# A four-block transformer kernel: residual with tokens on partitions, norms by bn_stats, key copies on ScalarE, and a new order

## The reference, cut to what matters

```
x = x + sigmoid(silu(c @ gate_w1) @ gate_w2) * (routed @ out_w)     # block 0, c = [norm(x), evidence, cond]
for each of blocks 1, 2, 3:                                        # eps, gates and biases differ
    n = ln(x) * (1 + scale_a) + shift_a                            # scale, shift, gate: one vector per sequence
    x = x + gate_a * (softmax(q(n) @ k(n).T * s) @ v(n) @ w_proj + b)
    x = x + (softmax(q(ln(x)) @ k(ctx).T * s) @ v(ctx) @ w_cproj + b)
    n = ln(x) * (1 + scale_m) + shift_m
    x = x + gate_m * (gelu(n @ w1 + b1) @ w2 + b2)                 # ln(t) = (t - mean) / sqrt(var + eps) over the 128 features
```

## Time and profile before

| | |
|---|---|
| median of 3 runs | 2806.82 us |
| the profiled execution, time | 2816.98 us |
| the profiled execution, span | 2815.2 us |
| granted TensorE clock, mean | 0.984 |
| instructions | 76312 |
| busy: PE / DVE / ACT / POOL | 2544.6 / 2204.7 / 1906.7 / 0.2 us |

### The profile page before, as it was taken

One profiled execution on the slowest core, in us unless ns is written; L12 is line 12 of the kernel. 1 busy time (PEld: TensorE's weight loads), 2 busy tenths in 40 slices (PEclk: granted clock), 3 DMA queues, 4 the chain that ended last, 5 costly groups with the idle time before them and its releaser, 6 DMA issues.

```text
span 2815.2 us, 76312 instructions
## 1 busy us (share of the span) xinstructions
PE 2544.6 (90%) x32150; PEld 1948.2 (69%) x32150; DVE 2204.7 (78%) x3752; ACT 1906.7 (68%) x3901; POOL 0.2 (0%) x4
## 2 busy tenths in 40 slices
PE   4989999999998999989999899989999898998997
PEld 3766777667766777667777667766777666776665
DVE  3788887788778887778877888777887778768785
ACT  2666667766676667767677666776667776777765
POOL 0000000000000000000000000000000000000000
PEclk9999999999999999999999999999999999999999
DMA  6100000000000000000000000000000000000000
GB/s 125 35 2 2 2 19 18 13 2 4 24 13 11 2 7 20 16 8 2 13 18 18 2 2 13 24 13 2 2 13 24 13 2 2 11 15 9 2 2 9
DMA packets 57963, 37.63 MB, mean 13 GB/s; under 512 B 20192, under 2 KB 52768, under 8 KB 57632
## 3 DMA queue, kind: packets, MB, share of 16 engines
q1 hardware_dynamic: 49120, 32.72, 4.1%
q10 hardware_dynamic: 8512, 0.03, 0.2%
HBM read 28.44 MB, written 4.29 MB: 12 GB/s over the span
## 4 chain that ended last, share of the span: by engine, by line
PE 59%; DVE 27%; ACT 8%; issue 3%; DMA 1%; DVEq 0%
PE pair L540 16%; PE pair L548 12%; PE pair L585 7%; DVE mx L731 7%; DVE wide L733 7%; PE pair L601 6%; PE pair L570 6%; PE pair L606 5%; PE pair L614 4%; DVE wide L727 3%; PE pair L555 2%; ACT vb L654 2%; ACT wide L661 2%; DVE xn L689 1%; DVE xn L691 1%
## 5 line engine op out<-in xcount | busy, mean ns | idle before, releaser
L585 PE MATMUL pair<-konst,wide 128*128 128x128 f32 x3072 | 404.5, 277 | 107.4 <-DVE wide L733 90.6
L661 ACT ACTIVATE wide<-pair 128x1024 f32<-128x1024 f32 x384 | 386.7, 1021 | 163.6 <-PE pair L585 162.3
L585 PEld LDWEIGHTS pair<-konst,wide 128*128 128x128 f32 x3072 | 347.6, 142 | 183.3 <-DVE wide L733 139.9
L731 DVE TENSOR_REDUCE mx<-pair 128x16 f32<-128x1024 f32 x320 | 389.3, 1216 | 49.3 <-PE pair L570 48.9
L733 DVE TENSOR_TENSOR wide<-pair,mx 128x1024 f32<-128x1024 f32 x320 | 391.8, 1224 | 10.9
L654 ACT ACTIVATE vb<-pair 64x128 f32<-64x128 f32 x768 | 207.6, 270 | 43.1 <-PE pair L555 26.5
L540 PE MATMUL pair<-wide,konst 128*128 128x256 f32 x704 | 218.4, 401 | 17.2 <-ACT wide L634 13.2
L570 PE MATMUL pair<-km,qT 32*64 32x256 f32 x6144 | 217.0, 390 | 17.6 <-DVE wide L733 7.1
L601 PEld LDWEIGHTS pair<-wide,vb 128*32 128x32 f32 x12288 | 183.9, 110 | 68.3 <-issue 29.0
L601 PE MATMUL pair<-wide,vb 128*32 128x64 f32 x12288 | 213.7, 221 | 11.0 <-ACT wide L661 9.2
L669 ACT ACTIVATE rec<-pair 128x256 f32<-128x256 f32 x192 | 73.7, 384 | 217.7 <-PE pair L606 217.3
(11 more groups left out here) (224 smaller groups left out, 4601.7 us busy)
## 6 DMA issues: line engine op xcount, KB each, us to landing
km<-probs_by_expert SPq DMA_DIRECT2D x32, 384.0 KB, 3.4
rows<-in_x_dram SPq DMA_DIRECT2D x32, 128.0 KB, 2.2
rows<-in_ctx_dram SPq DMA_DIRECT2D x32, 128.0 KB, 2.3
out_dram<-wide SPq DMA_DIRECT2D x32, 128.0 KB, 1.8
w0e<-in_L_xcond_e_w_dram SPq DMA_DIRECT2D x4, 384.0 KB, 5.7
w1fc<-in_L_xcond_fc_w_dram SPq DMA_DIRECT2D x2, 256.0 KB, 5.6
w2fc<-in_L_xcond_W_mlp_dram SPq DMA_DIRECT2D x2, 256.0 KB, 6.9
wide<-in_L_xcond_ffn_w_dram SPq DMA_DIRECT2D x2, 256.0 KB, 5.4
```

Of the source, the lines that this page charges most:

```text
L585: ins = pe.transpose(b[:, t:t + 128], G.ss[:, 2 * c + rr, a:a + 128], ident)
L661: act.activation(G.pT[:, :, 4 * c:4 * c + 4, :].rearrange("k p h q -> k p (h q)"), two_banks(name)[:].rearrange("k (p n) -> k p n", p=2), ...
L731: dve.tensor_reduce(top, heads(s), AX_X, ALU.max).then_inc(*tick("dve", ("max", G.n, tag, c)))
```

## The change

Four things change together.

**The residual has tokens on partitions.** `x` is now 128 tokens x 2 x 128 features, loaded and stored without any turn; only the context is still turned. There are two x buffers per stream. The cross projections, block 3's self projection and block 3's last MLP product swap their operands (`pe_token_product`), so that the result has tokens on partitions and is added to x from PSUM by one pass. Gated deltas are still made with features on partitions; a piece `bk` turns them back with two transposes ahead of the add. A bias along features can't ride on the add any more: for three of the adds GpSimd adds a bias row to x earlier, after the norm has read x.

**Norms by bn_stats.** VectorE takes mean and variance per token (two `bn_stats`, two `bn_aggr`), ScalarE takes logarithm and exponential of 128 x 2 numbers, VectorE subtracts and multiplies (two `tensor_scalar` over 128 columns), TensorE transposes twice, and ScalarE evicts: with scale and shift in four activations of 64 columns, one per sequence, or in one of 256 columns.

**Masked key copies on ScalarE.** Four activations of 256 columns with the mask as scale and the masked bias as bias.

**The order.** Most costs of the timetable are changed a little, a hop towards TensorE has its own length, GpSimd is an engine of the timetable, and each kind of piece has an offset on its rank from the table `ORDER` (some 200 numbers, of which one line stands below). In the order that comes out ScalarE has 241 table loads where it had 294.

```diff
 assert GI == NG
 PE_MM, PE_TURN, PE_SCORES, PE_MIX = 0.44, 0.12, 1.05, 1.95
-ACT_256, ACT_BIAS, ACT_SBUF, ACT_1024, ACT_VALUES, ACT_TABLE = 0.36, 0.45, 0.42, 0.96, 1.2, 1.3
-DVE_256, DVE_PTR, DVE_1024, DVE_MASK, DVE_SMALL = 0.36, 0.42, 1.16, 1.24, 0.2
-HOP, PE_HOP, LEAD = 0.07, 0.22, 12.0
+ACT_256, ACT_BIAS, ACT_SBUF, ACT_1024, ACT_VALUES, ACT_MODULATE, ACT_TABLE = 0.34, 0.43, 0.42, 0.95, 1.08, 1.0, 1.3
+POOL_ADD, ACT_KEYS = 0.8, 1.55
+DVE_256, DVE_PTR, DVE_1024, DVE_MASK, DVE_SMALL, DVE_TWO, DVE_STATS, DVE_APPLY = 0.36, 0.42, 1.195, 1.24, 0.16, 0.95, 0.75, 0.42
+HOP, TO_PE_HOP, PE_HOP, LEAD = 0.07, 0.16, 0.24, 11
+ORDER = {
+    "in": -8, "c in": -8.5, "pen": 54.5, "rstd0": 9.5, "ap0": 55, "nT0": 10, "xn0": 22,
...
-        rank = {p.name: p.name[0] * LEAD - left[p.name] for p in pieces}
+        rank = {p.name: p.name[0] * LEAD - left[p.name] + ORDER.get(p.name[1], 0.0) for p in pieces}
...
-                self.x, self.cT = own("x", [128, T]), own("cT", [128, T])
+                self.x = own(f"x{n // NS % 2}_", [128, TT, D])
+                self.ctx, self.cT = own("ctx", [128, TT, D]), own("cT", [128, T])
+                self.stats, self.mv, self.rstd = own("stats", [128, 2, TT, 6]), own("mv", [128, 2, TT, 2]), own("rstd", [128, 2, TT])
...
+        def pe_token_product(pe, name, pairs):
+
+            b = claim(pe, name)
+            for t in range(TT):
+                for i, (m, w) in enumerate(pairs):
+                    ins = pe.matmul(b[:, t * 128:(t + 1) * 128], m[:, t * 128:(t + 1) * 128], w, start=(i == 0), stop=(i == len(pairs) - 1))
+            ins.then_inc(*tick("pe", ("mm", name)))
+
...
+        def dve_stats(dve, G, tag):
+
+            x, stats, mv, _, _ = norm_of(G, tag)
+            for t in range(TT):
+                dve.bn_stats(stats[:, t, :], x[:, t, :]).then_inc(*tick("dve", ("stats", G.n, tag, t)))
+            for t in range(TT):
+                dve.wait_ge(*done("stats", G.n, tag, t))
+                dve.bn_aggr(mv[:, t, :], stats[:, t, :]).then_inc(*tick("dve", *([("var", G.n, tag)] if t else [])))
...
+        def dve_apply(dve, G, tag):
+
+            x, _, mv, rstd, out = norm_of(G, tag)
+            dve.wait_ge(*done("rstd", G.n, tag))
+            for t in range(TT):
+                dve.tensor_scalar(out[:, t, :], x[:, t, :], mv[:, t, 0:1], rstd[:, t:t + 1], ALU.subtract, ALU.mult)\
+                    .then_inc(*tick("dve", *([("normed", G.n, tag)] if t else [])))
+
...
+        def act_modulate(act, G, tag, scale, shift, dst):
+
+            name = (G.n, tag, "n")
+            act.wait_ge(*done("mm", name))
+            for q in range(GB):
+                seq = G.n * GB + q
+                act.activation(dst[:, q * S:(q + 1) * S], tile(name)[:, q * S:(q + 1) * S], ACT.Identity,
+                               scale=table[:, scale, seq:seq + 1], bias=table[:, shift, seq:seq + 1])\
+                    .then_inc(*tick("act", *([("free", name), ("xn", G.n, tag)] if q == GB - 1 else [])))
+
...
-        def dve_keys(dve, G, tag, bias):
-
-            mask = konst[:, K_MASK:K_MASK + JH].unsqueeze(2).broadcast_to((128, JH, T))
-            wide = lambda ap: ap.unsqueeze(1).broadcast_to((128, JH, T))
+        def act_keys(act, G, tag, bias):
+
+            masks = konst[:, K_MASK:K_MASK + JH]
+            name = (G.n, tag, "k")
             if bias is None:
-                dve.tensor_tensor(G.km[:], wide(G.kT[:]), mask, ALU.mult).then_inc(*tick("dve", ("km", G.n, tag)))
+                act.wait_ge(*done("kT", G.n, tag))
+                src = G.kT[:]
             else:
-                name = (G.n, tag, "k")
-                dve.wait_ge(*done("mm", name))
-                dve.scalar_tensor_tensor(G.km[:], wide(tile(name)[:, 0:T]), bias, mask, ALU.add, ALU.mult)\
-                    .then_inc(*tick("dve", ("free", name), ("km", G.n, tag)))
+                act.wait_ge(*done("mm", name))
+                src = tile(name)[:, 0:T]
+            for j in range(JH):
+                end = [("km", G.n, tag), *([] if bias is None else [("free", name)])] if j == JH - 1 else []
+                act.activation(G.km[:, j, :], src, ACT.Identity, scale=masks[:, j:j + 1],
+                               bias=0.0 if bias is None else kbias[:, 4 * bias + j:4 * bias + j + 1]).then_inc(*tick("act", *end))
...
+        def pool_bias(pool, G, which, ready, end):
+
+            pool.wait_ge(*done(*ready))
+            pool.tensor_tensor(G.x[:], G.x[:], bias_tok[:, which:which + 1, :].broadcast_to((128, TT, D)), ALU.add).then_inc(*tick("pool", ("biased", G.n, end)))
+
+        def dve_residual(dve, G, name, biased, end):
+
+            name = (G.n, *name)
+            if biased:
+                dve.wait_ge(*done("biased", G.n, end))
+            dve.wait_ge(*done("mm", name))
+            dve.tensor_tensor(G.x[:], tile(name)[:, 0:T].rearrange("p (t d) -> p t d", t=TT), G.x[:], ALU.add)\
...
-        def norm(G, tag, before, ready, scale, shift, dst, eps, src):
-
-            cen, var = (tag, "cen"), (tag, "var")
-            put_product(G, "cen" + tag, cen, PE_MM, [(center, src[:])], before, wait=[ready])
-            put(G, "sq" + tag, "act", ACT_256, lambda act: act_square(act, G, tag), "cen" + tag)
-            put_product(G, "var" + tag, var, PE_MM, [(average, squares(G, tag)[0])], "sq" + tag, wait=[("sq", G.n, tag)])
-            put(G, "rstd" + tag, "act", ACT_BIAS + ACT_SBUF, lambda act: act_rstd(act, G, tag, eps), "var" + tag, gives=[var], table=EXP_TABLE)
+        def norm(G, tag, before, ready, scale, shift, dst, eps):
+
+            def dve_first(dve):
+                if ready is not None:
+                    dve.wait_ge(*ready)
+                dve_stats(dve, G, tag)
+            put(G, "st" + tag, "dve", DVE_STATS, dve_first, *before)
+            put(G, "rstd" + tag, "act", 0.48, lambda act: act_rstd(act, G, tag, eps), "st" + tag, table=EXP_TABLE)
+            put(G, "ap" + tag, "dve", DVE_APPLY, lambda dve: dve_apply(dve, G, tag), "rstd" + tag)
+            put(G, "nT" + tag, "pe", 2 * PE_TURN, lambda pe: pe_turn_norm(pe, G, tag), "ap" + tag, takes=[((tag, "n"), 1)])
             if scale is not None:
-                put(G, "scale" + tag, "dve", DVE_256, lambda dve: dve_scale(dve, G, tag, scale, dst), "sq" + tag, gives=[cen])
-                put(G, "xn" + tag, "dve", 2 * DVE_256 + HOP, lambda dve: dve_norm(dve, G, tag, shift, dst), "rstd" + tag, "scale" + tag)
-            elif tag == "0":
-                put(G, "xn" + tag, "dve", 2 * DVE_256 + HOP, lambda dve: dve_norm0(dve, G), "rstd" + tag, gives=[cen])
+                put(G, "xn" + tag, "act", ACT_MODULATE, lambda act: act_modulate(act, G, tag, scale, shift, dst), "nT" + tag, gives=[(tag, "n")])
             else:
-                put(G, "xn" + tag, "dve", DVE_256, lambda dve: dve_norm(dve, G, tag, None, dst), "rstd" + tag, gives=[cen])
+                put(G, "xn" + tag, "act", ACT_BIAS if tag == "0" else ACT_256, lambda act: act_normed(act, G, tag, dst), "nT" + tag, gives=[(tag, "n")])
+
+        def add_gated(G, src, tag, before, ready):
+
+            def emit(pe):
+                pe.wait_ge(*done(*ready))
+                pe_turn_back(pe, (G.n, tag, "back"), src)
+            put(G, "bk" + tag, "pe", 2 * PE_TURN, emit, before, takes=[((tag, "back"), 1)])
+            put(G, "x" + tag, "dve", DVE_256, lambda dve: dve_residual(dve, G, (tag, "back"), False, tag), "bk" + tag, gives=[(tag, "back")])
...
-            put(G, "km" + tag, "dve", DVE_MASK + (3 * DVE_256 + HOP if L == 3 else 0), dve_k, "k" + tag, gives=[(tag, "k")])
+            if L == 3:
+                put(G, "kT" + tag, "dve", 3 * DVE_256 + HOP, lambda dve: dve_rotary(dve, G, tag, "k", G.kT, "kT"), "k" + tag, gives=[(tag, "k")])
+            put(G, "km" + tag, "act", ACT_KEYS, lambda act: act_keys(act, G, tag, bias), "kT" + tag if L == 3 else "k" + tag,
+                gives=[] if L == 3 else [(tag, "k")])
...
```

More of the change, by code:

```diff
@@ L440, in _ @@
                 pe.wait_ge(*done("router pad"))
-                pe.transpose(bank[7][:, 0:B], G0.x[:, 0:D], ident).then_inc(*tick("pe", ("cond",)))
+                pe.transpose(bank[7][:, 0:B], visits[NS].x[:, 0, :], ident).then_inc(*tick("pe", ("cond",)))
                 for n, (w, i) in enumerate(blocks):
@@ L503, in _ @@
                         .then_inc(*tick("dve", ("table", n)))
+                dve.wait_ge(*done("bias rows"))
+                dve.tensor_copy(bias_tok[:], bank[7][:, D:4 * D].rearrange("p (n d) -> p n d", n=3))
         nc.all_engine_barrier(sems_to_clear=counters)
@@ new lines, in pe_turn_norm @@
+        def pe_turn_norm(pe, G, tag):
+            pe.wait_ge(*done("normed", G.n, tag))
+            b = claim(pe, (G.n, tag, "n"))
+            out = norm_of(G, tag)[4]
+            for t in range(TT):
+                ins = pe.transpose(b[:, t * 128:(t + 1) * 128], out[:, t, :], ident)
+            ins.then_inc(*tick("pe", ("mm", (G.n, tag, "n"))))
+        def act_modulate(act, G, tag, scale, shift, dst):
```

(17 more changed lines are left out.)

230 lines of the change are left out of this document (118 added, 112 removed), and 33 rows, old and new, of the table ORDER.

## The result

The changed kernel took 2669.59 us (median of four runs, 2669.04 to 2674.36). The kernel before, run beside it on the same chip, took 2810.71. The ratio is 0.950, with a 95% interval of 0.9475 to 0.9526: 141 us less. The forecast was 2613, range 2530 to 2730.

The account below looks back on a forecast made before the run. The prediction took TensorE's work to bound the kernel. Set-up 57 + 1, TensorE 2323 and idle 240 gave a 2621 us span, 2623 executed, and 2613 as median by the factor 0.9964; range 2530 to 2730.

Parts of the forecast that it names:

- the second pointer: ScalarE modulation and biased keys: price shown by no row; perhaps another 0.09 us per activation, some 93 ns by the skill.
- I take 1.0: ScalarE modulation: a run of four 64-column activations costs 1.0 us, 224 us for 224 runs (208 to 289).
- the high ends: ScalarE with the scale pointer charged too: modulation run 1.29 us, keys 46 us more than 301, engine at 2230.
- The low end of 2070: ScalarE's total busy time after the change: 2070 us at the least, 2119 expected, 2230 at the most.
- The 240 of idle time: TensorE after the set-up: idle put at 240 us, where the old idle share of 8.4% would give 213.
- the gain is that the fullest engine sheds 204: TensorE: work is moved more than removed; the gain comes from TensorE losing 204 us, down to 2323.
- a saving on TensorE should therefore reach the time: Whole kernel: bound by TensorE's work, idle only 8.4%, so less of it shortens the time until the next engine stops it.
- Better packing: Order of work: offsets and freer PSUM banks cut TensorE's idle time to 140 us, 2513 us in all; chance 0.12.
- ScalarE becomes the limit: ScalarE at 2230 us: exponentials wait behind key copies and modulations, TensorE idle 380, 2753 us in all; chance 0.15.
- the signs of being wrong: ScalarE holding TensorE over 150 us, key runs near 2 us, VectorE awaiting GpSimd adds, TensorE falling much less than 204.
- Slower: Key copies ahead of the scores wait on ScalarE, 1.3 us for each of 192 attentions: 2853 us; chance 0.06.
- The change does not do what it says: TensorE: the two removed norm products ran in gaps, so gaps only widen: between 2795 and 2820 us; chance 0.05.

Follow-up runs that it names:

- Run 4: Changed kernel, same order, with the bias operand of modulation and biased key copies set to constant 0, so one pointer instead of two: 2616.85 us, 0.930.
- Run 8: Kernel before with its own arithmetic, but the change's waits and timetable costs, a fitted table of offsets and LEAD 92: 2693.67 us, 0.9575.
- run 9: Changed kernel with the key copies back on VectorE, costs as in the change's trace, offsets and LEAD fitted to that placement: 2683.49 us, 0.954.
- run 10: Changed kernel with the same work, timetable costs taken from its trace, offsets and LEAD fitted again: 2651.77 us, 0.943.
- run 12: Kernel before in its own order, with one more 128-column product per norm on TensorE, 78 us of added work: 2855.35 us, 1.015.
- run 1: Changed kernel with an empty table of offsets, its new costs and hops kept: 2770.6 us, 0.985.
- run 2: Changed kernel with the key copies back on VectorE in one pass, the change's offsets left, not fitted again: 2975.07 us, 1.057.

## Why the prediction was right, and where it was wrong

**Work on the engines: right but for ScalarE.** TensorE stands at 2329 us (forecast 2323), VectorE at 2064 (2058), and there are 241 table loads, as forecast. The statistics pass was taken at 0.279 and lasts 0.284; the aggregation 0.166 and 0.173. The apply pass was too low, 0.22 against 0.341; since neighbours overlap, the three kinds together cost 484.6 us and not 468, a miss of 17.

**The mis-sized term: the second pointer.** The step "I take 1.0" for a modulation run failed: it is 1.29, and a biased key run 1.93 instead of 1.57. Both are the high ends that the prediction had worked out and not taken. Modulation is 65 us over its term and the keys, 356.3 us instead of 301, 55 over. ScalarE as a whole is 58 over, and not 120, for the most part because instructions of different lines overlap: all its lines added up (1980.7 us before, 2318.2 after) exceed the engine's busy time by 74 us before and by 130 after, and the sum had no term for those 56. (The low end of 2070 that it gives for ScalarE does not follow from its terms, which give 2103; nothing rests on it.) The rule of the Trainium skill, page "ScalarE: Activation LUTs", section "What ACT_TABLE_LOAD costs", that each such pointer costs some 93 ns, was set aside as the high end; the trace agrees with it for both pointers, 384, 476 and 571 ns. Run 4 takes the second one out, and the time falls to 2617. The error of 57 us is not all from that: the pointer is worth 53 us of time, but ScalarE as a whole missed by 58, and at 0.45 of a microsecond for each that is 26. So by this estimate 26 to 53 of the 57 us are its doing. By terms of the sum the error is: idle time 286 instead of 240, TensorE 6 more, and 5 us from the factor between the profiled execution and the median, which was 0.998 and not 0.9964; 2613 + 46 + 6 + 5 = 2670. The 240 of idle time was a choice near the old idle share and not worked out, so what made up the rest stays open.

**The wrong step: "the gain is that the fullest engine sheds 204".** The size of the gain fitted, its cause did not. Run 8 has none of that saving and is 120 us faster than before. With fitted orders, the new norms and residual are worth 10 us with the keys on VectorE (run 9 against 8, intervals overlap) and 24 to 42 with them on ScalarE. The saving does arrive on TensorE: 2486.5 to 2318.1 us busy between runs 8 and 10. But its idle time goes from 145.5 to 273.9, and 128 of 168 us are given back. In run 8 TensorE is nearest to being the bound, with 67% of the chain and 94.5% busy, though no run adds work to it there; in run 10 three engines have 2318, 2149 and 2071 us in 2592. The premise "a saving on TensorE should therefore reach the time" was already true only in part: run 12 gives it 0.52 of the work added, 0.73 of the busy time.

**The rivals.** "Better packing" was named as a rider with a chance of 0.12, and against it was said that three full engines leave little slack. It was the main effect, 101 us in the change (run 1) and 120 in the kernel before (run 8). That it did not show as an idle time of 140 in the change because the new work on ScalarE and VectorE took it up is my reading of run 8's 145.5 us beside the change's 285.7; no run shows it by itself. "ScalarE becomes the limit" was half right: at 2177 us it takes 31% of the chain, but its sensitivity is 0.45 and not 1. Of the signs of being wrong, ScalarE held TensorE up for 131 us, under the 150 named, and VectorE waits for no GpSimd add; a key copy run "near 2 us" did come, 1.93 for the biased ones. "Slower" did not come about. "The change does not do what it says" gave no such time, but its mechanism, a saving that widens the gaps, is what runs 8 and 10 show for 128 of 168 us. The forecast came near by luck: one effect that was underrated, the order, and one that was overrated, the saving on TensorE, largely made up for each other.

**What stays open.** The shares of order and work depend on how far each search got. Whether run 8's or run 10's order is the best for its work isn't known, and their `LEAD` differs (92 and 14.5), though both have offsets in the thousands, so the 24 to 42 us may be off by what a longer search finds.

## What to carry to other kernels

Where a list order is fixed in advance, fit the order of the old work too before crediting a change of work; here the order alone gave 120 us where the whole change gave 141. Undoing one part without fitting again misleads: run 2 came out 162 us slower than the kernel before, and the same work with its own order, run 9, 132 us faster. And with several engines at about 80% or more, price an edit by its sensitivity, found by adding known work to one engine at a time: here 0.2 to 0.5 each after the change, not 1 for the fullest.
